# Decoder of two layers: the first attention's front reordered, and the choosing of tokens joined with the gated experts

## The reference

```
x_conv = x.transpose(0, 2, 1)
tau = sigmoid(conv1d(gelu(conv1d(x_conv, tau1_w, tau1_b, (1, 1), groups=D)), tau2_w, tau2_b))
delta = sigmoid(conv1d(gelu(conv1d(x_conv, del1_w, del1_b, (1, 1), groups=D)), del2_w, del2_b))
scores = scores * tau[..., None] + delta[:, :, None, :]
```

```
gates, idx = top_k(affinity, CAP)
h = gelu(einsum('becd,edf->becf', take(x, idx), w1) + b1)
out = out.at[batch, idx].add(gates * (einsum('becf,efd->becd', h, w2) + b2))
```

## Time and profile before

| | us |
|---|---|
| median of 3 runs | 2352.15 (2349.53 to 2354.15) |
| the profiled execution | 2349.88 |
| its span, first to last instruction | 2348.1 |
| TensorE busy | 2116.4 (90%) |
| VectorE busy | 1500.9 (64%) |
| ScalarE busy | 1271.5 (54%) |
| GpSimd busy | 1087.2 (46%) |

### The profile page before, as it was taken

One profiled execution on the slowest core, in us unless ns is written; L12 is line 12 of the kernel. 1 busy time (PEld: TensorE's weight loads), 2 busy tenths in 40 slices (PEclk: granted clock), 3 DMA queues, 4 the chain that ended last, 5 costly groups with the idle time before them and its releaser, 6 DMA issues. The chain is left out here.

```text
span 2348.1 us, 47594 instructions
## 1 busy us (share of the span) xinstructions
PE 2116.4 (90%) x17594; PEld 1476.4 (63%) x17594; DVE 1500.9 (64%) x2941; ACT 1271.5 (54%) x2070; POOL 1087.2 (46%) x1260
## 2 busy tenths in 40 slices
PE   7799999996995599979999979954999999999998
PEld 5466666663663488846666658832676676676675
DVE  5677777775996755547888746656555555555553
ACT  2377676663442355536666645443646646646643
POOL 2788888841220222136666214403455455455452
PEclk9899999997997799999999989976999999999999
DMA  5000000000002233211111000043344344345342
GB/s 231 1 2 1 0 0 0 0 1 7 9 7 72 99 131 137 87 42 36 27 27 27 1 13 21 11 144 110 79 111 109 76 110 109 75 111 110 74 83 28
DMA packets 66920, 136.03 MB, mean 58 GB/s; under 512 B 11200, under 2 KB 52368, under 8 KB 59920
## 3 DMA queue, kind: packets, MB, share of 16 engines
q1 hardware_dynamic: 37264, 87.65, 10.8%
q0 software_dynamic: 29568, 47.21, 10.1%
HBM read 100.22 MB, written 34.60 MB: 57 GB/s over the span
## 5 line engine op out<-in xcount | busy, mean ns | idle before, releaser
L3436 ACT ACTIVATE f_h<-bank,f_b 128x512 f32<-128x512 f32 x256 | 176.2, 688 | 275.2 <-PE bank L176 268.6
L176 PE MATMUL ring<-f_w2hi,f_hidhi 128*128 128x256 f16 x1024 | 280.0, 273 | 6.1 <-DVE f_hidlo L3479 3.8
L3479 DVE TENSOR_TENSOR f_hidlo<-f_h,f_hidhi 128x512 f16<-128x512 f32 x256 | 177.2, 693 | 166.5 <-ACT f_hidhi L3437 166.1
L176 PE MATMUL ring<-f_w2hi,f_hidlo 128*128 128x256 f16 x1024 | 279.9, 273 | 0.0
L176 PE MATMUL ring<-f_w2lo,f_hidhi 128*128 128x256 f16 x1024 | 279.9, 273 | 0.0
L3536 POOL DMA_INDIRECT out<-f_y,f_to_row x128 | 201.9, 1577 | 96.9 <-DVE f_y L3494 51.1
L176 PE MATMUL bank<-f_xthi,f_w1hi 128*128 128x512 f16 x512 | 194.1, 379 | 0.3 <-DVE f_xtlo L3457 0.3
L176 PE MATMUL bank<-f_xtlo,f_w1hi 128*128 128x512 f16 x512 | 194.0, 379 | 0.0
L176 PE MATMUL bank<-f_xthi,f_w1lo 128*128 128x512 f16 x512 | 194.0, 379 | 0.0
L3437 ACT ACTIVATE f_hidhi<-bank,f_b 128x512 f16<-128x512 f32 x256 | 174.4, 681 | 0.0
L3521 POOL DMA_INDIRECT f_xg<-tokens,f_from_row x128 | 149.9, 1171 | 47.9 <-issue 34.5
(11 more groups left out here) (631 smaller groups left out, 5987.8 us busy)
## 6 DMA issues: line engine op xcount, KB each, us to landing
f_raw<-in_e_w SPq DMA_DIRECT2D x32, 1024.0 KB, 5.5
c_raw<-in_e_w SPq DMA_DIRECT2D x16, 1024.0 KB, 5.6
slots_out<-c_y SPq DMA_DIRECT2D x40, 128.0 KB, 4.0
x<-in_x SPq DMA_DIRECT2D x1, 4096.0 KB
tokens<-c_xn SPq DMA_DIRECT2D x16, 256.0 KB, 2.6
tokens<-f_xn SPq DMA_DIRECT2D x16, 256.0 KB, 2.6
out<-x SPq DMA_DIRECT2D x1, 4096.0 KB, 15.2
wb<-in_wb SPq DMA_DIRECT2D x1, 3096.0 KB, 31.7
```

The source lines that it names most:

```text
L176: mm = pe.matmul(out, left[a], right[b], start=first and n == 0, stop=last and n == 2)
L3436: act.activation(h32[n % 4][:, :], src, ACT.Gelu_apprx_tanh, bias=bias).then_inc(sig["h_full"], 1)
L3479: dve.tensor_tensor(hid_v[1][:, it, at], h32[n % 4][:, :], hid_v[0][:, it, at], ALU.subtract).then_inc(sig["h_lo"], 1)
```

## The change

In the attention's front, ScalarE makes the first tap with its bias (`first_taps`) for the three parts that VectorE convolves, and VectorE adds the other two taps; each part waits for `first_tapped`. GpSimd casts the keys behind twin 1's part 1 and stacks the deltas behind its part 2. `keep_busy` has 10 matmuls there instead of 16.

`choose_tokens` is gone as a block. Its work is in the block of the experts, one group after the other: VectorE chooses and numbers group 0, takes its rows, and then does the same for group 1. A group's tiles are one half of every expert's rows. Numbers and gates are doubled before the transpose, so that one transpose lays them out for both halves of the partitions (`by_tile`, `chosen`). The loads of the first expert's weights stand at the block's beginning; its low parts are made on GpSimd (`first_parts`, `second_parts`) between the gathers of its halves (`gather_first`). TensorE does six hidden tiles of expert 0's first half before it turns the second half's rows, in banks 4 and 6. The other 15 experts go through `other_experts`, six turns of two and three written out. For every expert the first layer goes half by half, hidden tile `n` = 8 c + it in bank `n % 4`, and the outputs wait for `h_lo` half by half. SP's wait for the stored tokens moves to the Sinkhorn block.

```diff
+                    keep_busy(pe, mem, twins[1].ring_bank[1], 10)
                     for t in (1, 0):
...
+                        ins = act.activation(u.dw_v[:, c, :], u.xp[:, (c // 2) % 2, 0:S], ACT.Identity,
+                                             bias=mem.cols[:, dwb + c:dwb + c + 1],
+                                             scale=mem.cols[:, dwc + TAPS * c:dwc + TAPS * c + 1])
+                    ins.then_inc(sig["first_tapped"], 1)
                 def front(w, j, v):
...
+                    for part in range(1, 4):
+                        first_taps(w, part)
                     act.wait_ge(sig["first_convolved"], 3)
...
                     for part in range(4):
                         convolve(twins[1], j, part)
-                        if part == 0:
+                        if part == 1:
                             high_keys(w, j)
+                        if part == 2:
...
                     dve.wait_ge(u["x_pad_ready"], i.now)
-                    for k in range(TAPS):
+                    dve.wait_ge(sig["first_tapped"], part)
...
+                            ins = dve.scalar_tensor_tensor(out=out, in0=x, scalar=w, in1=out, op0=ALU.mult, op1=ALU.add)
...
+def other_experts(eng, count, step):
+    with eng.Fori(0, count // 2 - 2) as i:
+        for k in range(2):
+            step(1 - k, Turn(eng.snap(i * 2 + 1 + k), eng.snap(i * 2 + 2 + k)), 2)
+    for k in range(3):
+        step(1 - k % 2, Turn(count - 3 + k, count - 2 + k), 2 - k)
...
-            choose_tokens(nc, mem, affinity, rows, gates, stored)
-        gated_experts(nc, mem, dram, out, rows, gates)
+            sinkhorn(nc, mem, logits, affinity, stored)
+        gated_experts(nc, mem, dram, out, affinity, rows, gates)
...
+            @block.sync
+            def _(sp):
+                sp.wait_ge(stored, 16 * (B + 1))
...
-                            pe.wait_ge(sig["h_hi"], e.count(NH, k - 3) if k < 3 else e.before * NH)
...
+                def turn_tokens(g):
+                    pe.wait_ge(sig[f"token_ready{g}"], 1)
+                    pe.transpose(row_bank[g][:, 0:P], token[g][:, :], mem.const("ident")).then_inc(sig["rows_made"], 1)
+                    pe.wait_ge(sig[f"twice_ready{g}"], 1)
+                    pe.transpose(gate_bank[g][:, 0:P], twice[g][:, :], mem.const("ident")).then_inc(sig["gates_made"], 1)
...
+                def hidden(e, c, some):
+                    for it in some:
+                        n = IT * c + it
+                        if n >= 4:
+                            pe.wait_ge(sig["h_hi"], e.count(NH, n - 3))
+                        for h in range(KT):
+                            mm = split_product(pe, bank[n % 4],
+                                               [w[:, h, it * P:(it + 1) * P] for w in w1_v],
+                                               [x[:, h, c * HALF:(c + 1) * HALF] for x in xt_v], h == 0, h == KT - 1)
+                        mm.then_inc(sig["h_made"], 1)
+                def outputs(p, e):
                     pe.wait_ge(sig["w2_split"], e.now)
-                    pe.wait_ge(sig["h_lo"], e.count(NH, NH))
                     for ct in range(CT):
+                        if ct % GT == 0:
+                            pe.wait_ge(sig["h_lo"], e.count(NH, IT * (ct // GT + 1)))
                         pe.wait_ge(sig["y_read"], e.count(CT, max(ct - 3, 0)))
                         for it in range(IT):
                                                [w[:, it, :] for w in w2_v[p]], it == 0, it == IT - 1)
                         mm.then_inc(sig["y_made"], 1)
...
+                def turn_next(e):
+                    for c in range(GROUPS):
+                        turn_rows(Turn(e.now, e.now + 1), c, None)
...
+                    pe.wait_ge(sig["w1_free"], e.now)
+                    for c in range(GROUPS):
+                        pe.wait_ge(sig["xt_ready"], e.count(4, 2 * c + 2))
+                        hidden(e, c, range(IT))
+                    if more:
+                        turn_next(e)
+                    outputs(p, e)
...
+                def first_expert():
+                    e = Turn(0, 1)
+                    turn_tokens(0)
+                    keep_busy(pe, mem, bank[5], 30)
+                    turn_rows(e, 0, bank[0:2])
+                    turn_tokens(1)
+                    pe.wait_ge(sig["w1_free"], 1)
+                    pe.wait_ge(sig["xt_ready"], 2)
+                    hidden(e, 0, range(IT - 2))
+                    pe.wait_ge(sig["gates_read"], 2)
+                    turn_rows(e, 1, early_bank)
+                    hidden(e, 0, range(IT - 2, IT))
+                    pe.wait_ge(sig["xt_ready"], 4)
+                    hidden(e, 1, range(IT))
+                    turn_next(e)
+                    pe.wait_ge(sig["gates_read"], 4)
+                    outputs(0, e)
...
+                def take_gates(g):
+                    act.wait_ge(sig["gates_made"], g + 1)
+                    for d in range(2):
+                        act.activation(by_tile(gates, d, g), chosen(gate_bank[g], d), ACT.Copy
+                                       ).then_inc(sig["gates_read"], 1)
...
+                def first_expert():
+                    e = Turn(0, 1)
+                    high_w1(e)
+                    high_w2(0, e)
+                    take_gates(0)
+                    high_rows(e, 0)
+                    gelus(0, e, 0, range(IT - 2))
+                    high_rows(e, 1, early_bank)
+                    gelus(0, e, 0, range(IT - 2, IT))
+                    take_gates(1)
+                    gelus(0, e, 1)
+                    split_next(0, e)
...
+                def choose(g):
+                    src = affinity[:, g * S:(g + 1) * S]
+                    for r in range(CAP1 // 8):
+                        eight = slice(g * CAP1 + 8 * r, g * CAP1 + 8 * r + 8)
+                        order.step(dve.max(best[:, eight], src))
+                        order.wait()
+                        if r < CAP1 // 8 - 1:
+                            rest = left[r % 2][:, :]
+                            replaced = order.step(dve.match_replace(rest, best[:, eight], src, -1.0))
+                        order.step(dve.max_index(where[:, eight], best[:, eight], src))
+                        if r < CAP1 // 8 - 1:
+                            order.wait(replaced)
+                            src = rest
+                    order.wait()
+                def number_tokens(g):
+                    def doubled(t):
+                        return t[:, g * CAP1:(g + 1) * CAP1].unsqueeze(1).to_broadcast([P, 2, CAP1])
+                    order.step(dve.tensor_copy(tiles(token[g][:, :]), doubled(where)))
+                    order.wait()
+                    dve.tensor_scalar(token[g][:, :], token[g][:, :], mem.const("entry_base")[:, g:g + 1], None, ALU.add
+                                      ).then_inc(sig[f"token_ready{g}"], 1)
+                    dve.tensor_copy(tiles(twice[g][:, :]), doubled(best)).then_inc(sig[f"twice_ready{g}"], 1)
...
+                def take_rows(g):
+                    dve.wait_ge(sig["rows_made"], g + 1)
+                    for d in range(2):
+                        dve.tensor_copy(by_tile(rows, d, g), chosen(row_bank[g], d)).then_inc(sig["rows_read"], 1)
...
+                def low_hidden(e, c, some=range(IT)):
+                    at = slice(c * HALF, (c + 1) * HALF)
...
+                def first_expert():
+                    e = Turn(0, 1)
+                    choose(0)
+                    number_tokens(0)
+                    take_rows(0)
+                    choose(1)
+                    number_tokens(1)
+                    low_rows(e, 0)
+                    take_rows(1)
+                    low_hidden(e, 0, range(IT - 2))
+                    low_rows(e, 1, early_bank)
+                    low_hidden(e, 0, range(IT - 2, IT))
+                    low_hidden(e, 1)
+                    dve.wait_ge(sig["gates_read"], 4)
+                    finish(0, e, 2)
...
+                def first_parts():
+                    pool.wait_ge(sig["w1_hi"], 1)
                     settle(pool, sig)
+                    pool.tensor_tensor(w1[1][:, :], raw1[:, :], w1[0][:, :], ALU.subtract).then_inc(sig["w1_free"], 1)
...
+                def second_parts():
+                    pool.wait_ge(sig["w2_hi"], 1)
+                    settle(pool, sig)
+                    pool.tensor_tensor(w2[0][1][:, :], raw2[:, :], w2[0][0][:, :], ALU.subtract
+                                       ).then_inc(sig["w2_split"], 1)
+                    pool.wait_ge(sig["w2_split"], 1)
+                    pool.sem_inc(sig["w2_free"], 1)
...
+                def gather_first(c):
+                    half = slice(GT * c, GT * c + GT)
+                    pool.wait_ge(sig["rows_read"], 2 * c + 2)
+                    settle(pool, sig)
+                    pool.tensor_copy(from_row[:, half], rows[:, half]).then_inc(sig["from_first"], 1)
```

(59 more changed lines are left out.)

181 lines of the change are left out of this document (54 added, 127 removed).

## The result

The changed kernel takes 2322.58 us (median of 4 runs, 2321.31 to 2324.60) against 2351.36 for the one before on the same chip (4 runs, 2349.53 to 2354.15): a ratio of 0.9878 with a 95% interval of 0.9867 to 0.9890, 28.8 us less. The forecast was 2330 with a range from 2324.

The account below looks back on a forecast made before the run. From the first expert on, TensorE almost alone was taken as the bound, with idle time mostly elsewhere. Gains of 6.5 (front), 8.0 (first expert) and 7.4 (loop) sum to 21.9 us, giving 2328 profiled, 2330 median; range 2324 to 2340.

Parts of the forecast that it names:

- First expert: From the first MAX8 to expert 0's second layer: choosing and gathering by halves gains 8.0 us, bounds 3 and 10.3.
- a landing follows its last issue by 3.5: Expert 0's gathers: the rows land 3.5 us after the last issue, a figure from the earlier trace.
- the second half's wait: Expert 0's first layer: TensorE stands 2.6 us for the second half's gathered rows, landing at 1628.8.
- a cool TensorE: Expert 0's first layer: slow matmuls cost nothing, covered by expert 1's gather with 2.8 us of room.
- the cast that waits for the split: Group 0's numbering on VectorE waits for GpSimd's split of w1: 2.3 us, bounds 0 and 5.1.
- Rival 1: First expert: choosing and GpSimd shut each other out; it gains only 3, total 17, time 2335; chance 0.13.
- Loop: From expert 0's second layer to the end: waiting half by half gains 7.4 us, bounds 5.5 and 7.8.
- The waits: TensorE's idle time before the experts' second layers goes: 3.6 us in the loop, 2.13 in the last expert.
- The 1.67 for a cool tail: Last expert's second layer: without the stand before it, it takes 21.13 us instead of 22.80.
- Rival 3: First layers: successive tiles in neighbouring banks slow the gelus; at 0.15 us a tile, 2368; chance 0.04.
- Front: Front of the first attention: TensorE's 4.98 us wait for gelu goes; gain 6.5 us, bounds 3 and 8.
- Rival 4: First expert late by 6 and the front fails too: nothing changes, within 5 us, 2348; chance 0.05.

Follow-up runs that it names:

- experiment 3: Changed kernel plus thirteen unused matmuls in expert 0, eight ahead of group 1's transposes and five behind them; 2324.03 us, ratio 0.9881.
- experiment 4: Changed kernel plus two unneeded 1 MB loads beside the first gather, with expert 1's first weight load behind them; 2326.80 us, ratio 0.9895.
- experiment 6: Changed kernel with GpSimd splitting w1 behind the first half's gathers and w2 behind the second half's; 2323.33 us, ratio 0.9879.
- experiment 1: Changed kernel with every expert's second layer waiting at its start for all sixteen hidden tiles again; 2331.53 us, ratio 0.9916.
- experiment 5: Changed kernel with the deltas stacked behind twin 1's part 1, with the keys, instead of part 2; 2319.86 us, ratio 0.9866.

## Why the prediction was right or wrong

**First expert, predicted 8.0, measured 12.6: the step that failed.** Counted from the first MAX8:

| step (us) | predicted | measured |
|---|---|---|
| group 0's numbers read | 14.1 | 12.9 |
| its four gathers issued | 19.9 | 18.8 |
| landed | 23.5 | 20.6 at the latest |
| first hidden tile | 27.2 | 24.9 |
| second half's rows turned | 37.6, after a wait of 2.6 | 34.4, no wait |
| expert 1's gather, first issue | 39.3 | 36.7 |
| its last issue ends | 50.5 | 46.4 |
| second layer | 55.1 | 50.5 |

The gain lies above the upper bound of 10.3 too. The step that failed is "a landing follows its last issue by 3.5". It was taken from the row at 1629.74 in the earlier trace rows. That gather ran beside a load of expert 1's weights, which SyncE issued at 1623.08. The first half's, read the same way, landed 3.84 behind its fourth issue (1618.15 + 0.95, to the turn at 1622.94) beside the first expert's loads, at a DMA share of 1.01 from 1616 to 1622. In the changed kernel the first expert's weights load during the choosing, and expert 1's load, issued at 1596.95, keeps the share at 0.84 from 1599 to 1602 only; the last issue starts at 1603.18. The DMA share (next to last number) beside the row of 1629.74, in the kernel before, and beside the first gather of the changed kernel:

```profile
1625.00:1627.00 2.00, 2.00 (x6) 0.69 (x5) 0.64 (x1) 0.00 (x0) 0.95 (x1) 0.50 0.93 389
...
1602.00:1606.00 4.00, 3.96 (x19) 1.66 (x18) 3.90 (x17) 0.00 (x0) 3.68 (x3) 1.00 0.34 98
```

There a landing takes 1.76 (experiment 3), and 5.54 with loads put back (experiment 4). Eight issues in a row are not the reason: in experiment 3 the rows of expert 1's eight are turned 1.86 behind the last. Nor is a stretched issue needed: the four of experiment 4 took 0.94 to 1.01 each. The row carried a condition that the change removes. Put 1.76 for 3.5 into the forecast's sum and leave the rest: the second half's wait shrinks from 2.6 to 0.9, expert 1's gather is issued from 37.6, and the second layer starts at some 51.6 instead of 55.1.

The first hidden tile is another matter: its 2.3 us come from VectorE. By the forecast too it waited for the numbering of group 1, and that was done 2.6 earlier than forecast: 1.2 are group 0's numbers, mainly as `w1`'s split took 4.07, not 5.1, and the 0.8 for `w2`'s split fell away, as it ends at 1608.23, 0.27 behind the start of the cast. With a landing of 3.5 the tile would have come some 0.1 later (estimate: 1604.12 and 3.5, and 2.76 from landing to tile as in experiment 4). For the same reason the second half's last issue ended at 31.1, not 34.0; this alone, put into the forecast's sum, gives 52.1.

With both put in, the second half's rows are turned at 32.9 and TensorE's own work (13.6 to the end of the first layer in the forecast, then 2.18 for the turns at 1633.64) ends at 48.7, and the gather no longer sets the start. The forecast held a cool TensorE to be covered by the gather, and that was wrong too: the 36 matmuls took 9.62 instead of 7.8, and this 1.8 makes the 48.7 the measured 50.5. Keeping TensorE warm brings 1.4 us of it, until the gather ends last again (experiment 3). Expert 1's eight issues took 9.7 us instead of the 11.2 of the earlier trace rows; there one took 1.88 beside VectorE's split of `w2`, which in the changed kernel GpSimd has done before, and the next 1.42.

Right were the order of events, the cast that waits for the split (1.42 more than group 1's; 2.3 predicted), and MAX8 untouched by it. Rival 1 is refuted by the row at 1592.82. The Trainium skill ("SBUF — State Buffer", "Who interferes with whom") says that VectorE's and GpSimd's shared port pair is locked for a whole instruction and that VectorE takes part only with two SBUF inputs or in a two-port mode. The traces agree as far as they reach: MAX8 0.41 beside the split, an `f_hidlo` with two SBUF inputs 4.09 instead of 0.69 (experiment 6); in which mode the cast runs no row tells.

**Loop, predicted 7.4, measured 10.1: right mechanism, term mis-sized.** The waits were priced by the idle column at 3.6 + 2.13 = 5.7; experiment 1 gives 8.3. The column leaves out the overlap that each wait destroys (0.16 to 0.17 for each of the experts, 2.6 in sixteen), which the forecast put at nothing; the gain lies above its bound of 7.8. The 1.67 for a cool tail was counted as a consequence of the 2.13, and experiment 1 shows the same stand without it: it was gained in this comparison, but is not shown to follow from the wait, so that this part of the forecast came true by luck as far as the runs show. 8.3 and 1.67 make the 10.1 but for 0.1. Rival 3 is refuted: a first layer takes 20.72 over four neighbouring banks, 20.73 before.

**Front, predicted 6.5, measured 5.4.** As predicted, the keys' turn waits for `stack_deltas` (4.50 at 86.22), the convolution is done before the second `tau_delta` needs it, and the 4.98 vanish. GpSimd ran later than drawn, `stack_deltas` at 85.28 instead of 83.2, and the rows began at 88.87, not 87.1. Its input was there 6.8 us before that (78.47 in experiment 5), and putting it behind part 1 gains 3.5 us more.

**Sum.** 5.9 + 12.6 + 10.1 = 28.6. Of the 6.7 us missing in the forecast 4.6 are the first expert's and 2.7 the loop's; the first stretch gives 0.6 back. Rival 4, no change, is refuted by all three stretches.

## What to carry to other kernels

A duration read from the trace before holds under the load of its own row: look at the DMA share and at the other engines beside it, and ask whether the change takes that load away; where the trace has the same step both ways, the two are the bounds. Price a wait of a pipelined engine by the distance of starts with and without it, or by the lengthened layer in the chain, not by the idle column alone. A split that is moved out of the way of one instruction can stop another one, as in experiment 6: put it beside work that the trace shows undisturbed by it, here MAX8. Before one step is blamed for a whole miss, put its measured value into the sum and see how much of the miss goes away.

## What the runs showed of the hardware

TensorE's granted clock is not decided by the length of a stand alone. In the changed kernel it stood 1.71 and 1.08 us before expert 0, and the clock from 1610 to 1614 was 0.63; in experiment 6 it stood 1.68 and 1.08 us at the same place, behind the same thirty matmuls, and the clock of the 36 matmuls was 1.00. The changed kernel, then experiment 6:

```profile
1610.00:1614.00 4.00, 3.75 (x11) 1.48 (x12) 0.87 (x4) 1.27 (x2) 2.12 (x3) 0.63 0.75 293
...
1612.00:1620.00 8.00, 7.71 (x36) 3.46 (x36) 3.61 (x7) 6.09 (x10) 5.58 (x6) 1.00 0.53 188
```

Before the last second layer a stand of 2.13 us was followed by 0.51 in the earlier trace rows and by 1.00 in experiment 1. What tells these cases apart stays open; a term for a cool TensorE behind a stand of 2 us is a bound, not a forecast.
